# Attention scores as products of two rounded 32-bit parts in 64 rows, two row tiles of TensorE for alternating chunks of queries

## What is computed

```python
q = x @ W_q
latent_kv = (k + v) @ W_down_kv
k_rec = (latent_kv @ W_up_k).reshape(b, s, H, HD).transpose(0, 2, 1, 3)
scores = jnp.einsum('bhqd,bhkd->bhqk', qh, k_rec) / math.sqrt(d)
decay = jnp.exp(-LAMBDA_DECAY * jnp.abs(t[:, None] - t[None, :]))
scores = scores * decay[None, None, :, :]
attn = jax.nn.softmax(scores, axis=-1)
out = jnp.einsum('bhqk,bhkd->bhqd', attn, v_rec)
```

## Time and profile before

| | us |
|---|---|
| median of 3 runs | 1751.62 (1751.22 to 1751.84) |
| the profiled execution, own time | 1757.73 |
| its span | 1756.0 |
| TensorE matmul busy | 1650.1 (94%) |
| ScalarE busy | 1163.8 (66%) |
| VectorE busy | 613.8 (35%) |
| DMA, all 16 engines | 20.2% of their time, 104.68 MB |
| mean granted TensorE clock | 0.977 |

### The profile page before, as it was taken

How to read it: one execution, slowest core, us unless ns; L and a number is a source line. 1 busy time by engine, 2 the same in 40 slices (tenths; PEclk the granted TensorE clock), 3 DMA queues, 4 the chain that set the end, 5 groups by cost and what they waited for, 6 DMA issues and landing times. The chain is left out here.

```text
span 1756.0 us, 26320 instructions
## 1 busy us (share of the span) xinstructions
PE 1650.1 (94%) x8752; PEld 646.0 (37%) x8753; DVE 613.8 (35%) x1688; ACT 1163.8 (66%) x1330; POOL 59.9 (3%) x104
## 2 busy tenths in 40 slices
PE   7639999999999999999999999998899999999996
PEld 5502222222222222222222222223465565466454
DVE  5804324234143242341341111112344434534432
ACT  4428898988998987989988999998232232222210
POOL 1000000000000000000000000000000000000000
PEclk9969999999999999999999999999899999999998
DMA  7412122122222221222222111123110000100000
GB/s 193 120 64 72 64 76 78 62 75 74 72 74 65 77 73 59 73 79 72 73 62 81 50 44 58 55 87 78 31 37 24 32 16 24 36 12 24 13 12 14
DMA packets 104017, 104.68 MB, mean 60 GB/s; under 512 B 46576, under 2 KB 91376, under 8 KB 103712
## 3 DMA queue, kind: packets, MB, share of 16 engines
q1 hardware_dynamic: 103968, 104.08, 20.2%
HBM read 70.51 MB, written 33.55 MB: 59 GB/s over the span
## 5 line engine op out<-in xcount | busy, mean ns | idle before, releaser
L683 ACT ACTIVATE work<-ps 128x1024 f32<-128x1024 f32 x1024 | 993.9, 1025 | 139.7 <-DVE ps L511 73.4
L604 PE MATMUL ps<-stack 96*128 96x512 bf16 (+3 forms) x2432 | 552.3, 350 | 56.0 <-POOL work L475 32.1
L613 PE MATMUL ps<-work 128*32 128x512 f32 x4096 | 550.6, 610 | 0.0
L511 DVE TENSOR_TENSOR ps<-ps,small 128x128 f32<-128x128 f32 x512 | 153.1, 299 | 804.9 <-PE ps L604 804.9
L604 PEld LDWEIGHTS ps<-stack 96*128 96x128 bf16 x2432 | 189.4, 98 | 620.8 <-ACT work L683 252.2
L1568 PE MATMUL ps<-xT,stack 128*128 (+1 forms) x320 | 156.4, 612 | 1.5 <-PEq L430 1.5
L613 PEld LDWEIGHTS ps<-work 128*32 128x32 f32 x4096 | 81.3, 108 | 189.1 <-ACT work L683 112.0
L1576 PE MATMUL ps<-xT,stack 128*128 (+1 forms) x320 | 150.4, 592 | 0.0
L1591 PE MATMUL ps<-stack,work 128*128 128x256 f32 x640 | 141.3, 380 | 0.0
L1541 ACT ACTIVATE work<-ps 128x512 f32<-128x512 f32 x80 | 47.6, 595 | 135.5 <-PE ps L1568 135.3
L1591 PEld LDWEIGHTS ps<-stack,work 128*128 128x128 f32 x640 | 120.6, 190 | 15.8 <-issue 0.2
(11 more groups left out here) (119 smaller groups left out, 806.9 us busy)
## 6 DMA issues: line engine op xcount, KB each, us to landing
parts_dram<-part SPq DMA_DIRECT2D x64, 384.0 KB, 4.0
stack<-parts_dram SPq DMA_DIRECT2D x128, 192.0 KB
stack<-parts_dram SPq DMA_DIRECT2D x128, 128.0 KB
work<-in_L_attn_x SPq DMA_DIRECT2D x16, 512.0 KB, 5.0
stack<-parts_dram SPq DMA_DIRECT2D x128, 64.0 KB
attn_dram<-work SPq DMA_DIRECT2D x16, 256.0 KB, 14.0
work<-attn_dram SPq DMA_DIRECT2D x8, 512.0 KB, 3.9
out<-work SPq DMA_DIRECT2D x8, 512.0 KB, 3.0
```

Source lines behind the costliest of these rows:

```text
L511: nc.vector.tensor_tensor(own_block(s), own_block(s), dmask, ALU.mult).then_inc(s_["masked"], 1)
L604: m = nc.tensor.matmul(ps[:, half_of(s, half) + q0 // CH % 2, q0 % CH:q0 % CH + w], stack[0:ROWS, par, k, s * P:(s + 1) * P], stack[0:ROWS ...
L613: m = nc.tensor.matmul(ps[STRIP * c:STRIP * (c + 1), ACC + par], Vg[:, par, s], probs[:, probs_of(par, s), chunk(c)], start=s == 0, stop=s ...
L683: nc.scalar.activation(probs[:, probs_of(par, s), half * HALF:(half + 1) * HALF], src, ACT.Exp, scale=SCALE).then_inc(s_["exp_done"], 1)
```

## The change

Queries and keys are each cut into two parts, a value rounded to `float32r` and the rest, both of 32 bits. The four products of parts lie in 4 x 16 = 64 rows. `K_st` holds these 64 rows twice, in partitions 0 to 63 and 64 to 127; `Q_st` holds the even chunks of 512 queries in the lower 64 and the odd chunks in the upper 64. So the matmuls of neighbouring chunks use two row tiles of the array. A load becomes 16 DMAs, eight of 32 rows of 8 KB (keys) and eight of 32 rows of 4 KB (queries). The two buffers of `K_st` lie where `stack` lies, `Q_st` in `work`. A `prepare` has one cast and one subtraction less. The kernel's second way (`prologue_shifted`, `attention_shifted`), taken only where scores are too large, keeps the old form; the 32-bit input does not take it.

```diff
+TILE_ROWS = 4 * HD
+HALVES_DMAS = 16
...
+        K_st = nc.alloc_sbuf_tensor_at("K_st", [P, 2, 2, S], F32R, offset=stack_at)
+        Q_st = nc.alloc_sbuf_tensor_at("Q_st", [P, 2, 2, S // 2], F32R, offset=work_at + 4 * 3 * S)
...
+        halves_dram = nc.dram_tensor("halves_dram", [4, 2, B * H, HD, S], F32, kind="Internal").ap()
...
+def store_halves(sp, halves_dram, part, rows, c, which, done):
+
+    at = (c % 2) * (S // 2) + (c // 2) * CH if which == 0 else c * CH
+    cols = slice(at, at + CH) if isinstance(at, int) else bass.ds(at, CH)
+    for a in range(2):
+        dst = halves_dram[2 * which + a].rearrange("i h d s -> i (h d) s")[:, rows, cols]
+        sp.dma_start(dst.rearrange("i r s -> r i s"), part[:, which, a]).then_inc(done, 16)
+
+
+def load_halves(sp, K_st, Q_st, halves_dram, m, par, done):
+
+    for a in range(2):
+        keys = halves_dram[2 + a].rearrange("i h d s -> i (h d) s")[:, bass.ds(m * HD, HD)]
+        queries = halves_dram[a].rearrange("i h d s -> i (h d) s")[:, bass.ds(m * HD, HD)]
+        for g in range(2):
+            for i in range(2):
+                at = g * TILE_ROWS + 2 * HD * i
+                src = keys[i:i + 1].to_broadcast([2, HD, S])
+                sp.dma_start(K_st[at:at + 2 * HD, par, a, :].bitcast(F32), src).then_inc(done, 16)
+                src = queries[:, :, g * (S // 2):(g + 1) * (S // 2)]
+                sp.dma_start(Q_st[at:at + 2 * HD, par, a, :].bitcast(F32), src).then_inc(done, 16)
...
+            sp.wait_ge(xn_ready, NB)
+            load_halves(sp, K_st, Q_st, halves_dram, 0, 0, stack_in)
...
-                nc.vector.tensor_copy(pt[:, :, 0], split).then_inc(prep_link, 1)
-                dve.wait_ge(prep_link, 3 * k + 1)
-                nc.vector.tensor_tensor(split, split, pt[:, :, 0], ALU.subtract).then_inc(prep_link, 1)
-                dve.wait_ge(prep_link, 3 * k + 2)
-                nc.vector.tensor_copy(pt[:, :, 1], split).then_inc(prep_link, 1)
-                dve.wait_ge(prep_link, 3 * k + 3)
-                nc.vector.tensor_tensor(pt[:, :, 2], split, pt[:, :, 1], ALU.subtract).then_inc(prep_sb, 1)
+                nc.vector.tensor_copy(pt[:, :, 0].bitcast(F32R), split).then_inc(prep_link, 1)
+                dve.wait_ge(prep_link, k + 1)
+                nc.vector.tensor_tensor(pt[:, :, 1].bitcast(F32R), split, pt[:, :, 0], ALU.subtract).then_inc(prep_sb, 1)
...
-                        load_stack(sp, stack, parts_dram, n + 1, 1 - par, s_[f"stk{1 - par}"])
+                        load_halves(sp, K_st, Q_st, halves_dram, n + 1, 1 - par, s_[f"stk{1 - par}"])
...
-                for q0, w, q, k in score_pieces(s, half):
-                    m = nc.tensor.matmul(ps[:, half_of(s, half) + q0 // CH % 2, q0 % CH:q0 % CH + w],
-                                         stack[0:ROWS, par, k, s * P:(s + 1) * P],
-                                         stack[0:ROWS, par, q, q0:q0 + w], start=True, stop=True)
+                for q0, w, a in score_pieces(s, half):
+                    c = q0 // CH
+                    tile = slice(c % 2 * TILE_ROWS, (c % 2 + 1) * TILE_ROWS)
+                    at = c // 2 * CH + q0 % CH
+                    m = nc.tensor.matmul(ps[:, half_of(s, half) + c % 2, q0 % CH:q0 % CH + w],
+                                         K_st[tile, par, a, s * P:(s + 1) * P], Q_st[tile, par, a, at:at + w], start=True, stop=True)
...
-                        wait(pe, "stk" + str(par), (it + par) * (16 * STACK_DMAS))
+                        wait(pe, "stk" + str(par), (it + par) * (16 * HALVES_DMAS))
```

More of the change, by code:

```diff
@@ L9 @@
 BF16 = mybir.dt.bfloat16
+F32R = mybir.dt.float32r
 ALU = mybir.AluOpType
@@ L39, with aligned @@
 FLAGS = 936
+def aligned(at):
+    return (at + 31) // 32 * 32
 def emit(nc, io):
@@ L57, in emit @@
         w_unit = sb("w_unit", [P, 2, KD, P])
+        stack_at = aligned(nc.sbuf_base)
         stack = sb("stack", [P, 2, 4, S], BF16)
         part = sb("part", [P, 2, 2, 3, CH], BF16)
+        work_at = aligned(nc.sbuf_base)
         work = sb("work", [P, 17408])
+        K_st = nc.alloc_sbuf_tensor_at("K_st", [P, 2, 2, S], F32R, offset=stack_at)
+        Q_st = nc.alloc_sbuf_tensor_at("Q_st", [P, 2, 2, S // 2], F32R, offset=work_at + 4 * 3 * S)
         ps = ctx.enter_context(nc.psum_tensor("ps", [P, 8, CH], F32))
@@ L68, in emit @@
                       w_qk=w_qk, w_unit=w_unit, stack=stack, part=part, work=work, ps=ps,
-                      attn_dram=attn_dram, parts_dram=parts_dram)
-        prologue(**common, shifted=False)
+                      attn_dram=attn_dram, parts_dram=parts_dram, halves_dram=halves_dram, K_st=K_st, Q_st=Q_st)
+        prologue(**common)
         layer(**common, attend=attention)
@@ L79, in emit @@
             common["sem"] = lambda n: nc.alloc_semaphore("s_" + n)
-            prologue(**common, shifted=True)
+            prologue_shifted(**common)
             layer(**common, attend=attention_shifted)
@@ L117, in load_stack @@
             sp.dma_start(stack[row * HD:(row + count) * HD, par, kind, :], parts).then_inc(done, 16)
-def prologue(nc, io, sem, ident, xT, V_all, decay, small, w_qk, w_unit, stack, part, work, ps, parts_dram, shifted, **_):
+def store_halves(sp, halves_dram, part, rows, c, which, done):
[4 more added lines that the diff above has]
+        sp.dma_start(dst.rearrange("i r s -> r i s"), part[:, which, a]).then_inc(done, 16)
@@ L122, in prologue, with prologue_shifted @@
+def prologue_shifted(nc, io, sem, ident, xT, V_all, decay, small, w_qk, w_unit, stack, part, work, ps, parts_dram, **_):
     w_k = carve(work, 0, KD, D)
@@ L201, in _ @@
                     nc.gpsimd.tensor_copy(w_unit[:, :, :, :], w_qk[:, :, :, 0:P]).then_inc(w_set, 1)
-                if shifted and n >= NB - 4:
+                if n >= NB - 4:
                     if n == NB - 4:
```

789 lines of the change are left out of this document (489 added, 300 removed).

## The result

| | before | after |
|---|---|---|
| median of 4 runs each on one chip | 1751.73 us (1751.22 to 1754.92) | 2733.75 us (2730.45 to 2734.62) |
| profiled execution of after: own time, span | | 2733.9, 2732.2 us |
| mean granted TensorE clock of after | | 0.791 |

The changed kernel takes 1.560 times as long (95% interval 1.557 to 1.562). The forecast was 2705 us in a range of 2590 to 2880, so the result is 29 us, 1.1%, above it.

What follows compares the result with a forecast made beforehand. TensorE bounds the old kernel; loads on two engines would bound the new. Load 1 landing at 211, thirty loads 1815, stores 74 + 25, waits 12, tail 573: span 2710, own time 2712, median 2705 us, range 2590 to 2880.

Steps and rivals of the forecast that it cites:

- each copy goes to an engine of its own, always counted from the first: Loads: all 16 DMAs of a load go to the same two engines, 1,572,864 bytes each, 60.5 us a head.
- Rate: Loads: 26 GB/s for each of two engines, so 60.5 us a head; bounds 23.8 and 27 GB/s.
- The lower bound: Lowest rate of an engine during loads: 23.8 GB/s, from 540,672 bytes in a 23 us window; 66.1 us a load.
- Scores, weight loads, clock at nothing: TensorE in the heads: faster or slower scores, weight loads and a lower clock are covered by 26 us of slack a head.
- Stores: Stores on the two load engines: parts 6.2 us, 12 times, 74 us; finished pairs 1.8 us, 14 times, 25 us.
- Waits on SyncE: Three changes of the group of eight: loads wait for stores to land, about 4 us each, 12 us.
- Head 0: Prologue: first load issued at 80 us (between 78 and 89.5), head 0 starting at 148 us.
- Load 1: Second head's load: issued 2 us before head 0 starts at 148, landing at 211 us.
- The tail: From head 31's start to the end: 573 us, left as before.
- Rival 1: Loads spread over more engines and hidden under heads, ScalarE bounds, kernel faster: about 1610 us; 4%.
- rival 3: Loads and heads in turn, each load starting only after the head before is computed: about 3600 us; 3%.
- rival 4: Two engines, but faster on long rows: a load takes 56.5 us, stores hidden, about 2530 us; 6%.

Runs made afterwards that it cites:

- e1: The changed kernel with the 16 rows outermost and copies or parts inside, for keys and queries alike: 1651.7 us, 0.941 of before.
- e2: The changed kernel with the axes swapped for the queries alone, keys still in two copies of 16 rows: 2241.2 us (one run).
- e5: The changed kernel with each copy or part of 16 rows in its own DMA with an outer axis of four: 1796.4 us (one run).
- e4: The kernel before the change with the axes swapped for its DMAs of 48 and 32 rows: 1729.8 us, 0.986 of before.
- e3: The changed kernel with every score matmul issued twice into the same place: 2735.5 us (one run).
- e10: The changed kernel with DRAM rows of parts 10,496 bytes apart instead of 8,192, loads still on two engines: 2678.9 us (one run).
- e9: e1 with DRAM rows of parts 10,496 bytes apart instead of 8,192: 1643.3 us, 0.937 of before.
- e11: e4 with DRAM rows 6,400 bytes apart instead of 4,096: 1726.1 us, 0.985 of before.
- e7: e1 with two bf16 parts in place of the two float32r parts, halving the bytes of stores and loads: 1617.2 us (one run).
- e8: e1 with each projection cut into halves in two steps and VectorE's preparing one step later: 1658.5 us, 0.943 of before.

## Why the prediction came out right, and what was off

**Bound and mechanism: right.** The step "each copy goes to an engine of its own, always counted from the first" was read from a share of 0.13 and the sizes in the old trace. It held for the new kernel (0.13, 53 GB/s), for three other orders of the axes (e1, e2, e5) and in the old kernel (e4). The rule of the Trainium skill (DMA: Bandwidth & Descriptors, Why a DMA increments its semaphore by 16 and not by 1), that a DMA's engines are the largest number up to 16 that divides the slowest dimension of both sides, agrees with the shares of all five.

**Rate.** 26 GB/s taken, 26.2 measured; 60.5 us forecast, 60.0 found: 30 x 0.5 = 16 us too much. The Trainium skill's 27 GiB/s (DMA: Bandwidth & Descriptors, Specifications), against which I weighed it, would have made 2505 us; the trace was right to overrule it. 27 GB/s each, in e5, is the most that a stretch with a known count of engines shows. The lower bound had a slip: 540,672 bytes in the window's 23 us are 23.5 GB/s, not 23.8. The measured rate lies above either.

**Scores, weight loads, clock at nothing.** Right, and shown by e3: 223 us more work of TensorE cost 1.7 us, which one run does not tell from nothing.

**Stores: the term that was mis-sized.** "6.2 us, 12 times" and 1.8 us, 14 times, made 99 us. From 212.32 to 2154.64 are 1942.3 us, 30 loads of 59.98 us are 1799.4, and three group changes cost some 3.8 us each, 11.5; 131.4 us are left for the stores, 32 too many. The finished pair came out about as forecast (1.8 to 2.5 us for 1.8); the parts did not. The step scaled the old stores by their bytes, from the earlier trace rows, 1 KB pieces at a pitch of 4 KB. The new rows are 2 KB pieces at a pitch of 8 KB, and there the rate halves. With another pitch (e10) stores cost 7.4 us for a pair on the mean, and 8.0 had been forecast.

**Waits on SyncE**: three of some 3.8 us (3.5 against the mean of the other intervals with stores of parts), forecast three of 4. Right.

**Head 0**: at 151.8 us, forecast 148. The first load was issued at 85.5, not at 80, in the range given. Its cause is the stores once more, seen on another engine: in the prologue VectorE waits until a store has landed before it may write its tile again,

```profile
47.50 0.69 DVE L253 TENSOR_TENSOR work<-ps,decay 128x512 f32<-128x512 f32 x1 [8.10 <-DMA halves_dram<-work]
```

and with 10,496 bytes that wait is 5.5 us and the first issue comes at 78.2 in e10 and 76.9 in e9; head 0 of e10 starts at 144.0. Load 1 landed 60.5 us after head 0 started, forecast 63. The tail took 577.6 us, forecast 573; where its 4 us come from is open.

The differences: stores +32, rate -16, head 0 +4, load 1 -2.5, tail +4, together +22 us, which is the 22 us between the forecast span of 2710 and the measured 2732. The terms miss in both directions and cancel in part, so that the total came within 1.1% is in part luck. The other 6 of the 29 us are the step from the profiled execution to the median: I took off the 6.1 us by which the profiled execution of before lay above its median, and that of after lies on its own.

**Rival 1** did not happen, but e1 makes it happen, so its sum can be read: 1610 forecast for hidden loads, 1652 and with the other pitch 1643 measured. A plain head came out as priced or better (29.95 us for 30.4; exponentials at 0.93 us in place of 0.95). What was too small was the rest: each projection head costs 3.6 us more than a plain one, 12 times, 43 us, where I had written "some 12 us"; and head 0 starts at 106.8 us in place of some 96. Its condition, that four engines are enough, was too low as well: e5 still waited 106 us. Two other rivals were added up wrongly, which changes neither the range nor the forecast: in rival 3, 148 + 31 x 96.2 + 573 is 3703 us, not 3600, and in rival 4 hidden stores are the whole 99 us of the sum, not 50.

Set against each other with good loads and other pitches in both (two chips, on which before takes the same time within 0.1 us), the new scores are worth 1726.1 - 1643.3 = 83 us, 4.8% (e11 and e9). The change had a gain in it, and the order of two axes cost 1082 us (after against e1).

## What to carry to other kernels

A DMA share that stands at 2/16 or 3/16 for long is not an idle DMA: multiply the share by 16, and if it is a small whole number look at the outermost axis of the copy. A short axis (copies of a broadcast, parts of a number) belongs inside, the rows outside; for the same bytes that was 15 us in place of 60. When bytes are moved into another layout, price them by a row of the same piece size and the same pitch, and if the trace has none, take the range from the two rates that it does show.

## What the runs showed of the hardware that I had not expected

- **SyncE's queue is short.** The first DMAs of a load are issued 0.7 us apart, but once some seven are under way the engine stands in the issue instruction. Seven is an estimate: at the last issue of load 0, 122.4 us, the two engines had moved some 35 us x 52 GB/s = 1.8 of its 3.15 MB, and 1.3 MB are seven DMAs of the mean size. That it stands until one is done is my reading.

```profile
94.00 7.03 SPq L151 DMA_DIRECT2D K_st<-halves_dram  x1
...
2014.45 17.90 SPq L151 DMA_DIRECT2D K_st<-halves_dram  x1
```

  So a load on two engines holds back what SyncE has to issue behind it, for up to 18 us. Here nothing on the path stood behind it but the next load.
- **The pitch of rows in DRAM** halves the rate of writes already at 8 KB (385 to 180 GB/s, e1 and e9). For the reads of a load, whole rows, the two pitches do not differ: 210 GB/s in e1's window above, and 210 in e9 from 580 to 595 us.
- **Each of two DMA engines moves twice what each of sixteen moves** in the same load: 26 GB/s in after, 13 in e1. Spreading a load over eight times the engines made it four times as fast.
- **A 32-bit `float32r` matmul** of 512 columns takes as long as one in bf16 (e1 and e7 differ by 0.11 us for a pair and a block alike, so not by a price of each chunk), and two in different row tiles run side by side (0.43 us the pair, 0.66 in one tile). Its weight load is longer, 185 ns against 93.
- **Splitting a projection between the score blocks is not free.** Its two halves (e8) cost 0.2 us more on TensorE than the whole, and a pair of heads 0.57 us more, 7 us in twelve. Whether that comes from the change between forms of matmul was not tested.
